# Query and key projection of a banded attention: each product once, in halves, put in place by transfers

## The chip, the cores and the metric

One NeuronCore of a Trainium2 chip runs the whole program. The metric is the device time of one execution in microseconds (us); lower is better. The kernel before took 2152.45 us, the median of three runs (2148.47 to 2153.92).

## The reference, cut to what matters

Sixteen sequences of 256 tokens with 128 features pass through eight residual blocks: a banded attention, a feed-forward net with integer weights, a causal attention, the same net, a chunked attention, a net with 4-bit block quantisation, a low-rank attention, that net again. Only the first block is touched. It has 16 heads of 64 features and a rotary embedding on queries and keys:

```
def _apply_rope(x):                       # x: (b, head, s, 64)
    cos = tile(cos(ang), (1, 2)); sin = tile(sin(ang), (1, 2))   # 32 frequencies, twice
    x1, x2 = split(x, 2, axis=-1)         # features 0..31 and 32..63 of a head
    rot = concatenate([-x2, x1], axis=-1)
    return x * cos + rot * sin
y = hidden @ W.T + bias                   # projection to 16 * 64 = 1024 features
q, k = _apply_rope(proj(Wq, bq)), _apply_rope(proj(Wk, bk)); v = proj(Wv, bv)
scores = q . k / 8, kept where the key lies in a band of 128 behind the query
out = softmax(scores) @ v, merged, @ Wo.T + bo
```

So the first 32 features of a rotated head are x1*cos - x2*sin and the other 32 are x2*cos + x1*sin.

## The kernel before, in words

**Units.** A unit is one sequence in one block; UNITS lists 16 band units (0 to 15), then 16 each of causal, chunk, lowrank and end. A unit's work is cut into steps, and the steps into six stages: forward and finish (the feed-forward net that precedes an attention), operands (norm, transpose, projections), maxima (row scores and their maximum), back (scores again, exponential, product with the values), tail (division and output projection).

**Order.** Nothing is decided on the chip. `make_plan` (from L372) goes through the steps once when the program is built, with durations from `work` (L112), dependences from `needs` (L156), a settling time for each engine (SETTLE) and, for each engine, stage and kind of unit, a number in LEAD (L292) that says how far ahead a step may push in. What comes out is one fixed list for each engine (PE, ACT, DVE, POOL, and SP, which only issues transfers), walked in order. An instruction whose wait is not met holds all that stands behind it on its engine. The plan also says which of three PSUM slots of 1024 columns (SLOTS) each product of TensorE uses; a slot comes free when the step named by `released_by` has read it.

**Operands of a band unit** (`operand_steps`, L74). The 1024 features of queries and keys are eight chunks of 128 features, two heads each. For a chunk j, step ("qk", j) makes four products of 128 x 256 into one slot: the queries, the queries with the halves of each head exchanged (from a second, permuted copy of the weights), the keys, and the exchanged keys. Each product is three matmuls, since the weights and the tokens are split into a high and a low part (`mm_split`). DVE then does four SCALAR_TENSOR_TENSOR operations (L1242): add the bias, multiply by the cosine or by the signed sine, into one of two buffers of `rope_part`; then it waits for its own writes (L1248) and frees the slot. POOL adds the two products into `band_r` (L986), in float32, ready for the scores of the back stage. ACT copies that chunk to `band_rb` in bf16 (L1007, called from the step ("cast", j)), which the row scores of the maxima stage read. ("cast", j) stands two chunks behind ("qk", j) in the list (CAST_LAG). `band_r` holds two units (RING), `band_rb` one: the first cast of a unit waits for the last row score of the unit before it. The row scores wait for all eight casts.

**After that.** Six row score products ("score", 0 to 5), each followed by a maximum on DVE (L1201); POOL turns the maxima into three bf16 parts (L937 to L940), PE transposes them, ACT copies them (nmT). The back stage has four groups of four heads: scores with the mask and the maxima added, exponential on ACT (L1087), product with the values into `ctx_ps`. In `build`, every product and mask of PE is issued by one helper, L1327, so its rows are told apart by tile names and shapes.

**SP** issues nothing during the band units; later it writes and reads back the small attentions' stacked operands through DRAM, six transfers to `scratch` (L875, L878) and four from it (L887) for each unit.

**Setup.** Before the units, the weights are loaded into buffers that are still unused, and split: ACT copies them to the high part (L730 to L737) and DVE subtracts for the low part (L757). The queries' and keys' weights are two loads of 1 MB, band_qk_a and band_qk_b, and the plain and the permuted rows stand in both.

Of the kernel before, what the change touches and what calls it, by code (L numbers as in the profile page):

```python
# [7 lines left out]
F32R = mybir.dt.float32r  # L8
# [6 lines left out]
P = 128  # L15
# [24 lines left out]
QUANT_OPS = (range(0, 3), range(3, 6), range(6, 9))  # L40
CAST_LAG = 2
# [32 lines left out]
def operand_steps(kind):  # L74

    steps = norm_steps(None)
    if kind in CONSTANT:
        steps.insert(1, ("bias",))
    if kind == "band":
        steps.insert(0, ("st",))  # L80
        for j in range(CHUNKS + CAST_LAG):
            if j < CHUNKS:
                steps.append(("qk", j))
            if j >= CAST_LAG:
                steps.append(("cast", j - CAST_LAG))
        return steps + [("v", 0), ("v", 1)]
    return steps + [("qk", 0), ("rope",), ("cast", 0), ("cast", 1), ("stack",), ("v", 0)]
# [24 lines left out]
def work(kind, step):  # L112
# [43 lines left out]
def needs(u, step, eng):  # L156
# [3 lines left out]
    if eng == "pe":  # L160
# [12 lines left out]
        if kind == "band" and step == ("qk", 0) and u >= RING:  # L173
            yield u - RING, LAST_S["band"], "pe"
        if step == ("score", 0):
            yield (u, ("stack",), "sp") if kind in SMALL else (u, ("cast", CHUNKS - 1), "act")
# [22 lines left out]
    if eng == "dve":  # L199
# [4 lines left out]
        if name == "hid":  # L204
            yield u, ("ffn", step[1]), "act"
            if step[1] == 1 and u == BATCH:
                yield u - 1, ("qk", CHUNKS - 1), "pool"
# [8 lines left out]
        if name == "qk" and step[1] >= 2:  # L216
            yield u, ("qk", step[1] - 2), "pool"
        elif name == "qk" and u:
            yield u - 1, ("qk", CHUNKS - 2 + step[1]), "pool"
# [8 lines left out]
    if eng == "act":  # L228
        if name == "low":
            yield u, ("xT", step[1]), "pe"  # L230
        if name == "cast" and kind == "band":
            yield u, ("qk", step[1]), "pool"
# [16 lines left out]
    if eng == "pool":  # L249
# [18 lines left out]
        if step == ("qk", 0) and u >= RING:  # L268
            yield u - RING, LAST_S["band"], "pe"
        if name == "clear":  # L270
            yield BATCH - 1, LAST_V["band"], "pe"
        if name == "zero":
            yield BATCH - RING, LAST_S["band"], "pe"
    if eng == "sp" and name == "stack":
# [13 lines left out]
SETTLE = {"pe": 0.18, "act": 0.12, "dve": 0.1, "pool": 0.08, "sp": 4.0}  # L288
# [5 lines left out]
        "tail": {"band": -1.574, "causal": 26.104, "chunk": 10.753, "lowrank": -0.884},  # L294
        "finish": {"causal": -2.336, "chunk": -0.206, "lowrank": -0.262, "end": -0.693},
        "forward": {"causal": 9.636, "chunk": -0.478, "lowrank": 0.173, "end": -1.16},
        "operands": {"band": 4.447, "causal": 7.702, "chunk": 18.901, "lowrank": 57.299},
        "maxima": {"band": 15.183, "causal": -0.256, "chunk": 0.135, "lowrank": -1.548},
        "back": {"band": -2.437, "causal": -0.43, "chunk": -0.634, "lowrank": -1.541},
    },  # L300
    "act": {
        "tail": {"band": 53.895, "causal": 17.872, "chunk": 17.73, "lowrank": 16.182},
        "finish": {"lowrank": -10.956, "end": -33.98},
        "forward": {"causal": -0.537, "chunk": 17.288, "lowrank": 1.988, "end": 21.987},
        "operands": {"band": -1.911, "causal": -2.563, "chunk": -3.605, "lowrank": 4.31},
        "back": {"band": 0.035, "causal": -3.733, "chunk": 11.32, "lowrank": 7.631},
    },
    "dve": {
        "tail": {"band": 24.321, "causal": 37.26, "chunk": 2.316, "lowrank": -0.51},
        "finish": {"causal": -16.196, "chunk": -16.754, "lowrank": -16.243, "end": -0.226},  # L310
        "forward": {"causal": 0.613, "chunk": 33.846, "lowrank": 11.755, "end": -4.652},
        "operands": {"band": 33.419, "causal": -10.053, "chunk": 2.99, "lowrank": 16.104},
        "maxima": {"band": 32.94, "causal": 14.633, "chunk": 16.275, "lowrank": 22.45},
    },
    "pool": {
        "tail": {"band": 8.427, "causal": 6.479, "chunk": -24.474, "lowrank": 9.213},
        "finish": {"causal": -25.627, "chunk": -19.656, "lowrank": -10.06, "end": 52.839},
        "forward": {"causal": 8.336, "chunk": -6.534, "lowrank": 23.043, "end": 42.583},
        "operands": {"band": 1.34, "causal": -30.392, "chunk": 23.562, "lowrank": 10.007},
        "maxima": {"band": 33.498, "causal": 30.314, "chunk": 6.896, "lowrank": 39.8},  # L320
    },
}
PER_UNIT = 0.01


def released_by(u, step):
# [6 lines left out]
    if name == "qk" and small:  # L333
        return u, ("rope",), "dve"
# [48 lines left out]
def make_plan():  # L383
# [8 lines left out]
    while left:  # L392
# [33 lines left out]
        done[u, step, eng] = start + time + SETTLE[eng]  # L426
# [34 lines left out]
def build(nc, a, out):  # L461
    ctx = ExitStack()
    with ctx:
# [26 lines left out]
        bias_qk = sb("bias_qk", [P, CHUNKS, 4])  # L490
        band_qk = [sb(f"band_qk{i}", [P, CHUNKS, 4, P], F32R) for i in range(2)]
# [22 lines left out]
        rope_part = sb("rope_part", [P, 2, 2, 2, TOK])  # L514
        band_r = sb("band_r", [P, RING, CHUNKS, 2, TOK])
# [72 lines left out]
        band_sum = sem("band_sum")  # L588
        band_cast = sem("band_cast")
# [77 lines left out]
        st_qk = [stage(CHUNKS * 4 * P // 2), va_flat]  # L667
# [189 lines left out]
        with nc.Block() as block:  # L857

            @block.sync
            def _(sp):  # L860
                def front_half(u, step):
# [4 lines left out]
                    if step != ("stack",):  # L866
                        return
# [862 lines left out]
```

## Time and profile before

| | |
|---|---|
| runs, us | 2152.45, 2153.92, 2148.47 |
| profiled execution, us | 2152.07 |
| its span, first to last instruction, us | 2150.2 |
| mean granted clock of TensorE | 0.936 of full speed |
| busy, share of the span | PE 83%, DVE 63%, POOL 46%, ACT 38% |
| band units | about 33 to 830 us |

The profile comes from one execution; a PE row's busy time is the union of overlapping matmuls, so a mean of one says little about the pace, and a stretch of rows in the timeline says more. PEld is the weight load beside a matmul. Rows of stretches have, in this order: the stretch and its length in us, the busy us (and instructions) of PE, PEld, DVE, ACT and POOL, the granted clock, the transfers' share and GB/s. Rows of the timeline have start and length in us, and in brackets the idle time before, with what ended it. An "issue" in a chain is time in which nothing that the profile shows was waited for.

### The profile page before, as it was taken

The numbers are of one execution on the slowest core, as the hardware profiler recorded it, in microseconds if no ns is written. First come the engines' busy times: TensorE is split into PE (matmuls) and PEld (weight loads), VectorE is DVE, ScalarE is ACT, GpSimd is POOL, SyncE is SP. The second block draws the span as 40 slices with busy tenths as digits, with TensorE's granted clock in tenths as the row PEclk, the third lists the DMA queues.
The fourth block names the chain that finished last, engine by engine and source line by source line (L and its number), as shares of the span: only waits on it lengthen the run. The fifth ranks groups of instructions, "written<-read, shape, count | busy, mean of one in ns | idle before, by whom it ended". The sixth has DMA issues, their size and how long they took to land.

```text
span 2150.2 us, 51747 instructions
## 1 busy us (share of the span) xinstructions
PE 1789.7 (83%) x21261; PEld 1250.9 (58%) x21261; DVE 1345.8 (63%) x2753; ACT 808.8 (38%) x1303; POOL 978.6 (46%) x1362
## 2 busy tenths in 40 slices
PE   4899889999999998879999997777776778888883
PEld 4566565666666666655555555667665455555553
DVE  4555555555555543574555555677876788888873
ACT  2333333333333332324444444333333444444441
POOL 3333222333332222453333435689997455555543
PEclk9999999999999999989999999888998788888886
DMA  4000000000000000023333332233443223323310
GB/s 161 1 1 1 1 2 1 1 1 1 1 1 1 1 1 1 16 56 74 64 78 71 75 75 61 60 74 78 91 87 65 46 62 65 65 65 65 65 21 8
DMA packets 167465, 89.54 MB, mean 42 GB/s; under 512 B 9393, under 2 KB 165810, under 8 KB 166978
## 3 DMA queue, kind: packets, MB, share of 16 engines
q1 hardware_dynamic: 167010, 85.70, 18.4%
q8 instruction: 172, 2.82, 0.6%
q14 instruction: 59, 0.48, 0.1%
q0 software_dynamic: 224, 0.54, 0.1%
HBM read 46.36 MB, written 39.85 MB: 40 GB/s over the span
## 4 chain that ended last, share of the span: by engine, by line
PE 51%; DVE 27%; ACT 7%; POOL 7%; issue 6%; DVEq 0%; POOLq 0%; ACTq 0%
PE slots L1327 38%; DVE nmx L1201 12%; PE ctx_ps L1327 10%; DVE rope_part L1242 4%; ACT probs L1087 3%; DVE rope_part L1166 2%; PE slots L1615 2%; ACT ctxT L1007 1%; DVE ctxT L1303 1%; DVE rope_part L1167 1%; POOL xn L922 1%; PE slots L1394 1%; ACT band_va L1023 1%; POOL band_rb L645 1%; DVE band_r L1167 1%
## 5 line engine op out<-in xcount | busy, mean ns | idle before, releaser
L1087 ACT ACTIVATE probs<-slots 128x1024 f32<-128x1024 f32 (+1 forms) x416 | 356.1, 892 | 322.0 <-PE slots L1327 318.8
L1201 DVE TENSOR_REDUCE nmx<-slots 128x8 f32<-128x1024 f32 (+2 forms) x352 | 407.7, 1216 | 102.8 <-PE slots L1327 101.2
L1327 PE MATMUL slots<-band_r 64*64 64x64 bf16 (+4 forms) x5120 | 393.6, 263 | 80.5 <-DVE nmx L1201 41.7
L1327 PEld LDWEIGHTS slots<-band_r 64*128 64x128 bf16 (+2 forms) x5120 | 194.6, 120 | 254.3 <-issue 129.8
L1242 DVE SCALAR_TENSOR_TENSOR rope_part<-slots,bias_qk,rope_band 128x256 f32<-128x256 f32 x512 | 212.3, 477 | 197.3 <-PE slots L1327 176.4
L1327 PE MATMUL ctx_ps<-probs,band_va 64*32 64x64 f32 (+4 forms) x5120 | 260.5, 313 | 42.3 <-issue 19.4
L986 POOL TENSOR_TENSOR band_r<-rope_part 128x512 f32<-128x512 f32 x128 | 164.5, 1285 | 250.9 <-DVE rope_part L1242 250.9
L1327 PE MATMUL slots<-mask,ident_bf 128*128 128x256 bf16 (+1 forms) x896 | 217.2, 324 | 46.9 <-DVE nmx L1201 17.7
L1327 PE MATMUL slots<-nmT,pick 64*128 64x256 bf16 (+2 forms) x2560 | 218.7, 241 | 2.7 <-issue 2.7
L1327 PEld LDWEIGHTS ctx_ps<-probs,band_va 128*32 128x32 f32 (+2 forms) x5120 | 145.3, 118 | 125.6 <-issue 62.8
L900 POOL TENSOR_TENSOR var_eps<-mean_var,eps 128x2 f32<-128x2 f32 x128 | 29.2, 228 | 393.4 <-DVE mean_var L1129 393.4
L1327 PE MATMUL slots<-xT,band_qk 128*128 128x256 f32 x1536 | 200.0, 288 | 8.2 <-DVEq L1248 6.1
L1327 PEld LDWEIGHTS slots<-xT,band_qk 128*128 128x128 f32 x1536 | 188.0, 191 | 19.7 <-DVEq L1248 13.6
L1007 ACT ACTIVATE ctxT<-ctx_ps 128x512 f32<-128x512 f32 (+1 forms) x112 | 87.4, 781 | 169.2 <-PE ctx_ps L1327 169.2
L922 POOL TENSOR_SCALAR band_va<-x,mean_var,rstd 128x128 f32<-128x128 f32 x128 | 100.8, 794 | 86.0 <-PE slots L1368 65.9
L1007 ACT ACTIVATE band_rb<-band_r 128x512 bf16<-128x512 f32 x128 | 79.4, 630 | 157.0 <-POOL band_r L986 157.0
L1327 PEld LDWEIGHTS slots<-mask,ident_bf 128*128 128x128 bf16 x896 | 54.9, 97 | 133.8 <-issue 44.9
L1166 DVE SCALAR_TENSOR_TENSOR rope_part<-band_va,slots 128x352 f32<-128x352 f32 (+2 forms) x128 | 68.6, 536 | 81.9 <-ACT band_va L1023 55.5
L1327 PEld LDWEIGHTS slots<-nmT,pick 64*128 64x128 bf16 (+1 forms) x2560 | 102.9, 104 | 11.5 <-issue 2.9
L922 POOL TENSOR_SCALAR xn<-x,mean_var,rstd 128x128 f32<-128x128 f32 x128 | 103.6, 816 | 2.9 <-POOL rstd L901 2.8
L937 POOL CAST nm<-nmx 128x64 bf16<-128x64 f32 x64 | 15.1, 236 | 179.0 <-PE slots L1573 92.7
L901 POOL TENSOR_TENSOR rstd<-var_eps,minus_half 128x2 f32<-128x2 f32 x128 | 91.5, 715 | 10.0
(181 smaller groups left out, 2947.5 us busy)
## 6 DMA issues: line engine op xcount, KB each, us to landing
band_r<-scratch SPq DMA_DIRECT2D x192, 192.0 KB, 4.5
scratch<-parts SPq DMA_DIRECT2D x96, 192.0 KB, 2.2
scratch<-parts SPq DMA_DIRECT2D x96, 128.0 KB, 2.1
scratch<-parts SPq DMA_DIRECT2D x96, 64.0 KB, 1.8
x<-in_x SPq DMA_DIRECT2D x16, 128.0 KB, 4.5
out<-x SPq DMA_DIRECT2D x16, 128.0 KB, 1.8
band_r<-in_band_qk_a SPq DMA_DIRECT2D x1, 1024.0 KB, 6.4
band_va<-in_band_qk_b SPq DMA_DIRECT2D x1, 1024.0 KB, 10.3
```

The costliest lines, as they stand in the source:

```text
L900: link(nc.gpsimd.tensor_tensor(var_eps[:, b], mean_var[:, b, :, 1], eps[:], ALU.add))
L901: nc.gpsimd.tensor_tensor(rstd[:, b], var_eps[:, b], minus_half[:], ALU.pow).then_inc(rstd_ready, 1)
L922: nc.gpsimd.tensor_scalar(xn[:, t, :], x[:, b, t, :], mean_var[:, b, t, 0:1], rstd[:, b, t:t + 1], ALU.subtract, ALU.mult).then_inc(xn_rea ...
L986: nc.gpsimd.tensor_tensor(band_r[:, b % RING, j], part[:, 0], part[:, 1], ALU.add).then_inc(band_sum, 1)
L1007: return nc.scalar.activation(dst, src, ACT.Copy)
L1087: nc.scalar.activation(probs[:, g % 2, step[2], :, 0:width], slot(u, step).rearrange("p (a n) -> p a n", a=2)[:, :, 0:width], ACT.Exp, sca ...
L1166: link(nc.vector.scalar_tensor_tensor(g_out, t_in, 1.0, gate, ALU.add, ALU.mult))
L1167: nc.vector.tensor_tensor(h_out, g_out, up, ALU.mult).then_inc(free_sem(u, ("ffn", i)), 1)
L1201: nc.vector.tensor_reduce(dst, src, axis=AX.X, op=ALU.max, negate=True).then_inc(free_sem(u, step), 1)
L1242: nc.vector.scalar_tensor_tensor(rope_part[:, c % 2, rot, qk, :], slot(u, step)[:, o:o + TOK], bias_qk[:, j, 2 * qk + rot:2 * qk + rot + 1 ...
L1327: return nc.tensor.matmul(o, lhsT, rhs, start=start, stop=stop, skip_group_check=shared)
L1615: last = nc.tensor.transpose(B[:, g * P:(g + 1) * P], ctxT[:, g, t * P:(t + 1) * P], ident[:])
```

## The change

**Weights and products.** The chunk of 128 features gives way to a quad of four heads (QUADS is 4). For a quad m, ("qk", m) makes four products into one slot: the first halves of the four heads' queries (4 x 32 = 128 features), the same of the keys, then the second halves of the queries and of the keys. The permuted copy of the weights is gone; the weights are one load of 1 MB.

**Rotation.** A new step ("rot", m) follows ("qk", m). In ("qk", m) DVE makes x1*cos and x2*sin and POOL subtracts; in ("rot", m) DVE makes x2*cos and x1*sin from the same slot and POOL adds. Each has four DVE operations and one of POOL, as a chunk had. The slot is freed after ("rot", m), so after eight DVE operations. POOL writes to a new buffer `quad_r`, for two quads, with 32 partitions for the half of one head.

**Transfers.** The halves lie on the wrong partitions: a head's first half belongs on partitions 0 to 31 or 64 to 95 of `band_r`, its second half 32 further. After each POOL operation, SP issues four SBUF to SBUF transfers (32 partitions, 2 KB each, 64 KB a transfer) that put them there. They count on a semaphore of their own for each of the two quad buffers. For a unit from the third on, the first half's transfers of a quad wait until the back scores S of that same group of four heads, two units earlier, have been issued by PE and are complete; before, POOL's first chunk waited for the last such group.

**Waits.** POOL reuses a quad buffer when that buffer's eight transfers of two quads before have landed. ACT's cast now covers a quad (128 x 1024), waits for its eight transfers, and stands two quads behind.

**Plan.** `work`, `needs` and `released_by` describe the new steps, SP gets 2.55 us for each group of four transfers and its own landing times (LANDS), and all 82 numbers of LEAD and PER_UNIT are new. So the lists of all five engines are drawn anew, for the other kinds of units as well, whose code is unchanged.

```diff
-        for j in range(CHUNKS + CAST_LAG):
-            if j < CHUNKS:
-                steps.append(("qk", j))
-            if j >= CAST_LAG:
-                steps.append(("cast", j - CAST_LAG))
+        for m in range(QUADS + CAST_LAG):
+            if m < QUADS:
+                steps += [("qk", m), ("rot", m)]
+            if m >= CAST_LAG:
+                steps.append(("cast", m - CAST_LAG))
...
-        "qk": [("pe", 1.43), ("dve", 1.56), ("pool", 1.21)] if big else [("pe", 0.72 if low else 1.43)],
+        "rot": [("dve", 1.56), ("pool", 1.29), ("sp", 2.55)],
+        "qk": [("pe", 1.43), ("dve", 1.56), ("pool", 1.29), ("sp", 2.55)] if big else [("pe", 0.72 if low else 1.43)],
-        "cast": [("act", 0.52)] if big else [("act", 0.52), ("pool", 1.1)],
+        "cast": [("act", 0.95)] if big else [("act", 0.52), ("pool", 1.1)],
...
-SETTLE = {"pe": 0.18, "act": 0.12, "dve": 0.1, "pool": 0.08, "sp": 4.0}
+SETTLE = {"pe": 0.18, "act": 0.12, "dve": 0.1, "pool": 0.08}
+LANDS = {"stack": 4.3, "qk": 1.4, "rot": 1.4, "res": 1.4}
 LEAD = {
     "pe": {
-        "operands": {"band": 4.447, "causal": 7.702, "chunk": 18.901, "lowrank": 57.299},
-        "maxima": {"band": 15.183, "causal": -0.256, "chunk": 0.135, "lowrank": -1.548},
+        "operands": {"band": 20.005, "causal": 1.174, "chunk": 24.896, "lowrank": 76.144},
+        "maxima": {"band": 0.021, "causal": 0.721, "chunk": 4.511, "lowrank": -1.567},
...
-PER_UNIT = 0.01
+PER_UNIT = 0.0286
...
+                    if kind == "band" and step[0] in ("qk", "rot"):
+                        m, second = step[1], step[0] == "rot"
+                        quad = b * QUADS + m
+                        sp.wait_ge(band_sum, 2 * quad + second + 1)
+                        if b >= RING and not second:
+                            sp.wait_ge(back_full, BACK_NO[u - RING, ("S", m, EXP_FILLS[kind] - 1)] + 1)
+                        for i in range(4):
+                            to = 64 * (i % 2) + 32 * second
+                            sp.dma_start(band_r[to:to + 32, b % RING, 2 * m + i // 2],
+                                         quad_r[32 * i:32 * i + 32, quad % 2, second]).then_inc(band_moved[quad % 2], 16)
...
                         pool.wait_ge(part_ready, 4 * (n + 1))
-                        if b >= RING and j == 0:
-                            pool.wait_ge(back_full, last_exp(u - RING) + 1)
+                        if quad >= 2:
+                            pool.wait_ge(band_moved[quad % 2], 128 * (quad // 2))
                         part = rope_part[:, n % 2]
-                        nc.gpsimd.tensor_tensor(band_r[:, b % RING, j], part[:, 0], part[:, 1], ALU.add).then_inc(band_sum, 1)
+                        nc.gpsimd.tensor_tensor(quad_r[:, quad % 2, second], part[:, 0], part[:, 1],
+                                                ALU.add if second else ALU.subtract).then_inc(band_sum, 1)
...
-                        act.wait_ge(band_sum, b * CHUNKS + j + 1)
+                        act.wait_ge(band_moved[quad % 2], 128 * (quad // 2 + 1))
...
-                        copy(band_rb[:, j], band_r[:, b % RING, j]).then_inc(band_cast, 1)
+                        copy(band_rb[:, 2 * m:2 * m + 2], band_r[:, b % RING, 2 * m:2 * m + 2]).then_inc(band_cast, 1)
...
+                        for sine in range(2):
                             for qk in range(2):
-                                o = 512 * qk + TOK * rot
+                                at = 2 * (second ^ sine) + qk
...
+                        if second:
+                            dve.wait_ge(part_ready, 4 * (c + 1))
+                            dve.sem_inc(free_sem(u, ("qk", m)), 1)
...
-                        pe.wait_ge(band_cast, (b + 1) * CHUNKS)
+                        pe.wait_ge(band_cast, (b + 1) * QUADS)
```

## Rows read from the trace of the kernel before

**Rows 1.** The page: each engine's busy us, share of the span, instructions.
```profile
PE 1789.7 (83%) x21261; PEld 1250.9 (58%) x21261; DVE 1345.8 (63%) x2753; ACT 808.8 (38%) x1303; POOL 978.6 (46%) x1362
```

**Rows 2.** Busy time by stretch: all band units, the rest, two single units.
```profile
33.00:830.00 797.00, 734.46 (x6694) 502.29 (x6696) 422.06 (x913) 258.06 (x397) 241.00 (x295) 0.99 0.00 1
890.00:2150.00 1260.00, 999.23 (x14144) 703.65 (x14143) 876.12 (x1727) 524.84 (x861) 701.26 (x1006) 0.90 0.30 63
...
204.50:261.05 56.55, 50.77 (x448) 34.39 (x444) 31.13 (x68) 16.96 (x27) 15.42 (x19) 0.94 0.01 1
...
472.00:522.52 50.52, 47.33 (x444) 32.38 (x440) 26.15 (x57) 16.75 (x27) 15.36 (x19) 1.00 0.00 1
```
**Rows 3.** The timeline of PE: projection of queries and keys, one unit.
```profile
472.00 8.99 PE L1327 MATMUL slots<-xT,band_qk 128*128 128x256 f32 x72
481.18 1.69 PE L1327 MATMUL slots<-xT,band_qk 128*128 128x256 f32 x12 [0.19 <-DVEq L1248]
483.05 1.68 PE L1327 MATMUL slots<-xT,band_qk 128*128 128x256 f32 x12 [0.18 <-DVEq L1248]
```

**Rows 4.** The chain of waits in order of time, from this unit's row scores on.
```profile
491.59 0.94 PE slots L1327 x10
...
492.63 4.63 DVE nmx L1201 x4
...
505.51 6.69 PE slots L1327 x60
512.20 2.24 PE ctx_ps L1327 x32
...
519.63 3.39 PE slots L1327 x30
```

**Rows 5.** Groups of instructions, 110 to 890 us: count, busy us, mean ns.
```profile
L1242 DVE SCALAR_TENSOR_TENSOR rope_part<-slots,bias_qk,rope_band 128x256 f32<-128x256 f32 x438 | 181.7, 477 | 174.4 <-PE slots L1327 156.6 <-DVE rope_part L1242 17.8
...
L986 POOL TENSOR_TENSOR band_r<-rope_part 128x512 f32<-128x512 f32 x111 | 142.6, 1285 | 220.1 <-DVE rope_part L1242 220.1
...
L1007 ACT ACTIVATE band_rb<-band_r 128x512 bf16<-128x512 f32 x111 | 68.7, 630 | 123.9 <-POOL band_r L986 123.9
```

**Rows 6.** The timeline: DVE's pace over two chunks in one unit.
```profile
155.75 1.66 DVE L1242 SCALAR_TENSOR_TENSOR rope_part<-slots,bias_qk,rope_band 128x256 f32<-128x256 f32 x4 [11.80 <-PE slots L1327]
...
157.62 1.66 DVE L1242 SCALAR_TENSOR_TENSOR rope_part<-slots,bias_qk,rope_band 128x256 f32<-128x256 f32 x4 [0.21 <-DVE rope_part L1242]
```

**Rows 7.** Waits of PE, 472 to 522.5 us: us, times, longest.
```profile
PE ctx_ps L1327 <- ACT ctxT L1007: 0.7, 1, 0.7
...
PE slots L1327 <- DVE nmx L1201: 0.4, 2, 0.2
...
PE slots L1327 <- DVEq L1248: 0.4, 2, 0.2
```

**Rows 8.** SP's transfers by line: ns of one issue, smallest, median, largest.
```profile
L875 SPq DMA_DIRECT2D scratch<-parts x144: 360/489/1875, 878.5 to 2037.5; - x144
...
L887 SPq DMA_DIRECT2D band_r<-scratch x192: 537/617/1665, 925.0 to 2047.4; - x192
```

**Rows 9.** The page's transfer issues: count, KB each, median us to landing.
```profile
band_r<-scratch SPq DMA_DIRECT2D x192, 192.0 KB, 4.5
...
scratch<-parts SPq DMA_DIRECT2D x96, 64.0 KB, 1.8
```
**Rows 10.** Busy time by stretch, after and around a gap of PE.
```profile
235.00:238.00 3.00, 1.08 (x14) 0.59 (x10) 0.51 (x3) 1.02 (x1) 2.66 (x6) 1.00 0.00 0
238.00:241.00 3.00, 2.28 (x26) 1.36 (x25) 1.34 (x3) 1.25 (x3) 0.53 (x1) 0.87 0.00 0
241.00:245.00 4.00, 3.80 (x17) 1.67 (x15) 1.57 (x3) 0.00 (x0) 0.00 (x0) 0.50 0.02 4
245.00:248.00 3.00, 3.00 (x19) 3.00 (x20) 0.00 (x0) 1.02 (x1) 0.00 (x0) 0.66 0.00 0
```

**Rows 11.** The setup, DVE's timeline: the second load's low part.
```profile
15.88 2.29 DVE L757 TENSOR_TENSOR band_qk<-band_va,band_qk 128x2048 fp32r<-128x2048 f32 x1 [1.39 <-ACT band_qk L734]
```

More of the change, by code:

```diff
@@ L40 @@
 QUANT_OPS = (range(0, 3), range(3, 6), range(6, 9))
+QUADS = HEADS // 4
 CAST_LAG = 2
@@ L172, in needs @@
             yield u, ("low", False), "dve"
-        if kind == "band" and step == ("qk", 0) and u >= RING:
-            yield u - RING, LAST_S["band"], "pe"
         if step == ("score", 0):
-            yield (u, ("stack",), "sp") if kind in SMALL else (u, ("cast", CHUNKS - 1), "act")
+            yield (u, ("stack",), "sp") if kind in SMALL else (u, ("cast", QUADS - 1), "act")
         if name == "nm":
@@ L303 @@
[L303 to L306, printed above, removed]
+        "tail": {"band": 35.697, "causal": 34.402, "chunk": 10.557, "lowrank": 26.695},
+        "finish": {"lowrank": -5.609, "end": -20.226},
+        "forward": {"causal": 13.82, "chunk": 38.078, "lowrank": -16.965, "end": 37.732},
@@ L307 @@
+        "operands": {"band": 1.828, "causal": -3.97, "chunk": -2.376, "lowrank": 8.411},
+        "back": {"band": -29.994, "causal": -5.221, "chunk": 4.729, "lowrank": -20.078},
     },
     "dve": {
[L309 to L312, printed above, removed]
@@ L313 @@
-        "maxima": {"band": 32.94, "causal": 14.633, "chunk": 16.275, "lowrank": 22.45},
+        "tail": {"band": -1.733, "causal": 60.397, "chunk": 5.011, "lowrank": 19.119},
+        "finish": {"causal": -48.899, "chunk": -28.059, "lowrank": 0.492, "end": -16.236},
+        "forward": {"causal": -4.349, "chunk": 70.344, "lowrank": 25.847, "end": -54.899},
+        "operands": {"band": -2.503, "causal": -6.955, "chunk": 5.379, "lowrank": 33.812},
+        "maxima": {"band": -2.962, "causal": -51.183, "chunk": 30.291, "lowrank": 36.608},
@@ L314 @@
     },
     "pool": {
[L316 to L320, printed above, removed]
-    },
-}
-PER_UNIT = 0.01
+        "tail": {"band": -42.083, "causal": 40.938, "chunk": 0.066, "lowrank": 6.629},
@@ L326, in released_by, with settles @@
+        "finish": {"causal": -27.454, "chunk": -49.756, "lowrank": 9.302, "end": 76.825},
+        "forward": {"causal": 1.399, "chunk": -20.38, "lowrank": 19.311, "end": 52.875},
+        "operands": {"band": 6.442, "causal": -8.743, "chunk": 50.085, "lowrank": 11.974},
+        "maxima": {"band": 8.799, "causal": 24.457, "chunk": -6.764, "lowrank": 62.179},
+    },
+}
+PER_UNIT = 0.0286
+def settles(step, eng):
+    return LANDS[step[0]] if eng == "sp" else SETTLE[eng]
 def released_by(u, step):
@@ L588, in build @@
         band_sum = sem("band_sum")
+        band_moved = [sem(f"band_moved{i}") for i in range(2)]
         band_cast = sem("band_cast")
@@ L685, in build @@
         }
-        def qk_half(part, i):
-            half = CHUNKS // 2
-            return band_qk[part][:, i * half:(i + 1) * half].rearrange("p a b c -> p (a b c)")
         def loaded(eng, *names):
```

91 lines of the change are left out of this document (43 added, 48 removed).

## The prediction

> **What bounds the kernel now.** I read first the busy shares, then busy time by stretch, then PE's timeline and the chain inside one unit. The page puts PE at 83% of the span and DVE at 63% [rows 1], but that averages unlike stretches. In the 797 us of the band units PE is busy 734.5 us (92%), DVE 422 (53%), POOL 241, ACT 258; in the 1260 us from 890 on PE is busy 79% and DVE 70% [rows 2]. So PE sets the pace in the first part, and in the second no single engine does. Most band units repeat to 0.02 us: from 421 to 725 us six periods of 50.5 us follow each other, and the one from 472.00 has PE busy for 47.33 us of 50.52, DVE for 26.15, at full clock [rows 2]. Three units that also carry the quantisation of the 4-bit weights are longer, the one from 204.50 by 6 us.
>
> Inside a period the reader is to see two things. The projection is one solid block of PE: 72 matmuls in 8.99 us, then twice 12 in 1.69 us behind a wait of 0.19 for a slot that DVE frees [rows 3], from 472.00 to 484.73, 12.7 us in all. Six chunks of 12 matmuls in 8.99 us are 1.50 us a chunk. And the chain runs over DVE only in this block and in the row scores, where 0.94 us of PE are followed by 4.63 us of maxima; from 505.5 to the period's end it is PE alone, back to back [rows 4]. What PE does less is therefore time won, as long as something else is ready to be put in its place.
>
> **Products removed.** Half the matmuls of the projection go: 4 quads x 12 in place of 8 chunks x 12, 16 units x 48 = 768 in all. The block of 12.7 us becomes 4 x 1.50 = 6.0 us of PE work [rows 3], so a period can shorten by 6.7 us at most, 107 us over 16 units. That is the bound of the gain in the band units.
>
> **DVE, POOL, ACT.** DVE makes as many operations of the same shape as before, 32 a unit at 0.477 us; POOL eight of 1.285 us, now four subtractions among them, which I price as the additions; ACT four casts of 1024 columns in place of eight of 512 at 0.630 us [rows 5]. Two of the old make 1.26 us, which bounds the new cast above, and one, 0.63, bounds it below; I take 1.05 us, so ACT gains about 0.8 us a unit. ACT is idle two thirds of a period [rows 2], so that is worth nothing. DVE's pace stays 1.87 us for each four operations, 155.75 to 157.62 [rows 6], 15.0 us for a unit. This is now 2.5 times PE's 6.0 us, where it was 1.2 times: the products can no longer be issued in one block, PE has to do about 9 us of other work between them. The back stage of the unit before offers enough: a period has 47.3 - 6.7 = 40.6 us of PE work, of which 34.6 is not this projection.
>
> **New hand-overs.** Breaking the block up costs small waits. The rows show what one is worth: 0.2 us for a slot released by DVE, 0.7 us for a `ctx_ps` bank that ACT copies out, at most [rows 7]. A quad holds its slot for eight DVE operations, 3.7 us, where a chunk held it for 1.7, so with three slots one or two are left for the back stage while the rotation runs. I take four more waits of 0.2 and one of 0.7, 1.5 us a unit. Below it is 0 (the planner finds an order without them), above it is the 6.7 us that is gained. So 6.7 - 1.5 = 5.2 us a unit is won, and a period becomes 45.3 us.
>
> **Transfers.** Each unit gets 8 groups of 4 transfers on SP, 512 in all, 33.6 MB. SP has nothing else to do in the band units; behind these transfers stand only the later ones of the same kind. An issue holds SP for 0.489 us (to DRAM) or 0.617 us (from it, more descriptors) in the median, 0.36 to 1.88 in all [rows 8]. I take 0.6: a group is 2.4 us and a unit 19.7 us by the larger median, 11.5 by the smallest row, 60 by the longest. At 19.7 SP is busy 43% of the new period, but inside the rotation it is slower than DVE (15.0 us). A 64 KB transfer to DRAM landed 1.8 us after issue, 192 KB in small rows from DRAM after 4.5 [rows 9]; SBUF to SBUF isn't in the trace, and I take 2.1, near the nearer row in size, with 0.6 and 4.5 as ends. The first sum is done 1.5 + 0.2 + 1.9 + 1.3 = 4.9 us after the first product starts; then 19.7 us of issues, 1.5 until the last has landed and a cast of 1.05 make 27 us to the first row score, where it was 491.59 - 472.00 = 19.6 [rows 3, 4]. That is 7.5 us more latency, and it costs nothing while PE has the unit before to work on: in those 27 us it needs 27 - 6.0 - 3.3 (two value projections of 1.66 us) = 18 us of other work, and the period has over 25 left without the row scores. With that cover gone it would cost 7.5 us a unit. If the transfers land late by 1 us, ACT waits in front of its exponentials; half of that might reach PE, one time a unit: 0.5 us, inside the 1.5 above.
>
> The trace shows what a real hole would add: where PE was busy only 1.08 of 3 us, the granted clock stood at 0.87, then 0.50 and 0.66 in the next stretches before it was back at 1.00, that is 1.2 GHz for some 6.8 us with PE busy throughout [rows 10]. Those matmuls took up to twice their time, so it cost up to 3.4 us. The Trainium skill (TensorE: Matmul & The Clock Gate, HAM oscillation) says that waits which come back in each round of a loop can throttle the array again every time. By that rule a transfer wait in every unit would pay those 3.4 us every time, 51 us over 15 units; by the periods of before, at 1.00 with no gap over 0.7 us [rows 2, 7], nothing. I keep it out of the sum and make it a rival (F).
>
> **Start.** One load of 1 MB, ACT's copy and DVE's subtraction of 2.29 us with 1.39 us of waiting before it fall away [rows 11]. They stand on the way to the first unit: 2.3 to 3.7 us, I take 3. The first unit has no unit before it to hide the longer rotation, so I count its 5.2 us as not won; the other 15 units count.
>
> **Later units.** Their code is unchanged but all lists are drawn anew. PE has 1260 - 999 = 261 us idle there [rows 2]; nothing in the trace says whether the new order has more or less. I take 0 and, as bounds, 2% of the stretch either way, 25 us.
>
> **The sum.** 15 x 5.2 + 3 = 81 us. The profiled execution took 2152.07 us with a span of 2150.2, 0.4 us from the median of 2152.45: 2152 - 81 = 2071 us.
>
> **Rivals.** A, the forecast: PE sets the pace, a period of 44.5 to 47 us; 2045 to 2100.
> B, the longer rotation is only partly covered. For it: SP and DVE both outlast PE in this block, and three slots are few. Against it: 25 us of other work are there. If a third of the 7.5 us shows, 2.5 us a unit, the gain is 15 x 2.7 + 3 = 43, 2109 us (2095 to 2130).
> C, more than forecast: no new waits (6.7 us a unit, 100 + 3) or a better order later: 2049 from the first alone, 2035 with some of the second.
> D, slower: SP becomes the bound. One mechanism: each unit needs 32 issues in order, and rotation can't run ahead by more than two quads. From 50.5 / 32 = 1.58 us an issue on, SP alone takes longer than the period of before. By the longest row of the loads, 1.665 us, it would be 53.3 us, 15 x 2.8 = 42 us more, 2191. Against it: medians of a third of that.
> E, the change doesn't shorten the period, because DVE's chain of 15.0 + 6.9 (maxima) and the waits between them set it already: 2149. Against it: PE is busy 94% of the period and the last 17 us of the chain are PE alone.
> F, the clock: PE waits once a unit for a cast whose transfers are late, long enough for the clock to fall as it did after the gap of before: 3.4 us at the most in each of 15 units [rows 10], on top of the forecast: 2122. Against it: such a gap has to be several times as long as any in a steady unit now. (It is the rule of the clock page above.)
>
> **How the numbers follow.** A 0.65, B 0.13, C 0.10, D 0.07, F 0.03, E 0.02. This kernel's runs differ by up to 0.3%, 6.5 us; less can't be told from no change. The range of 2038 to 2120 takes all of A, two thirds of B and most of C; it leaves out D, E, F and the rest, some 0.18. Faster by over 0.3%: A, B, C and F, 0.91; within 0.3%: E, 0.02; slower: D, 0.07.
>
> **What would show it.** In the profile of after: 768 matmuls on band_qk in groups of 12, each 1.5 us apart from other PE work; a steady period near 45.3 us with PE busy about 41 and the clock at 1.00; SP issues of 0.5 to 0.65 us, 512 of them, landing in 1.5 to 2.5 us; POOL waiting for transfers seldom; the first row score some 27 us behind the first product of its unit. Wrong would be: a period above 47 us with PE idle for a cast or a slot (B), issues above 1.5 us (D), a stretch after the last band unit whose length differs from before by more than 25 us, or a clock below 1.00 in the steady units.

## The result, and the profile after

The changed kernel takes 2123.3 us (median of 2124.22, 2130.74, 2122.37 and 2122.23), against 2152.42 before: a ratio of 0.9869, 95% interval 0.9848 to 0.9891. Faster by 1.3%, where 3.8% was forecast, and 3 us above the range.

The page of after, to be read against [rows 1]: PE is busy for 58 us less, and its clock is lowered in the first two slices, where the page of before has 9. (In the later units it is lowered in both, and a 9 is anything from 0.90 on, so this row can't show the 0.93 to 0.96 of the band units below.)

```profile
span 2122.0 us, 50629 instructions
...
PE 1731.3 (82%) x20493; PEld 1184.8 (56%) x20493; DVE 1345.2 (63%) x2752; ACT 788.8 (37%) x1238; POOL 972.0 (46%) x1362
...
PEclk8799999999999999999999999987877788888897
```

Time went where the tiles' first starts show it. PE's rows of the projections of two kinds of unit, in the trace of before and then of after (min/median/max ns, first and last start):

```profile
L1327 PE MATMUL slots<-xT,causal_qkv x192: 276/281/387, 857.7 to 1244.0; 128*128 128x256 f32 x192
...
L1327 PE MATMUL slots<-xT,lowrank_qkv x96: 274/281/562, 1610.9 to 2023.8; 128*128 128x256 f32 x96
```
```profile
L1342 PE MATMUL slots<-xT,causal_qkv x192: 276/280/387, 828.6 to 1211.6; 128*128 128x256 f32 x192
...
L1342 PE MATMUL slots<-xT,lowrank_qkv x96: 277/281/553, 1571.0 to 2000.6; 128*128 128x256 f32 x96
```

The first causal unit starts 29.1 us earlier. From there to the end of the span before has 1292.5 us and after 1293.4, so the new order of the later units is worth nothing in sum (they win 11 us up to the first lowrank unit and lose them again). 2.8 of the 29.1 us are the setup, and 26.3 the band units. The same stretch, first product to first causal product, in busy time by engine (stretch and length, busy us of PE, PEld, DVE, ACT, POOL, clock, transfers); first before, then after, and after's first 67 us alone:

```profile
33.13:857.70 824.57, 755.12 (x6847) 519.20 (x6847) 436.24 (x950) 265.04 (x413) 251.95 (x311) 0.99 0.00 1
33.13:103.37 70.24, 61.58 (x487) 43.12 (x487) 42.43 (x86) 21.81 (x32) 28.99 (x34) 1.00 0.00 1
```
```profile
30.37:828.60 798.23, 684.62 (x6107) 445.62 (x6107) 436.05 (x950) 252.95 (x351) 249.56 (x311) 0.93 0.18 43
30.37:97.04 66.67, 36.91 (x184) 24.70 (x184) 35.18 (x80) 12.93 (x15) 27.68 (x30) 0.73 0.27 64
```

This is the whole account. PE lost 768 matmuls of 0.125 us (1.50 us for 12), 96.0 us of work, but its busy time fell by only 70.5. The other 25.5 us, a remainder, I put down to matmuls at the lower clock: in e9 below, whose steady units are at 1.00, PE is busy 684.1 us in this stretch with 240 added matmuls of about 0.11 us, so some 658 without them, and there the 96 us are gone in full. And PE's idle time rose from 69.5 to 113.6 us, by 44.2. 96.0 - 25.5 - 44.2 = 26.3 us. Half of the new idle time, 21.1 us, lies in the first two units; the other 14 have 23.1, or 1.65 us each.

**A steady unit after.** It takes 47.56 us (50.52 before), with PE busy 42.28 at a clock of 0.96 where [rows 2] had 47.33 at 1.00. The projection is no block any more: three quads, the first back scores of an older unit, the fourth quad, then the rest of that back stage. PE's timeline, cut to the ends of its parts (561.75 is the first row score of the unit whose projection began at 487.39):

```profile
534.95 4.50 PE L1342 MATMUL slots<-xT,band_qk 128*128 128x256 f32 x36
540.06 0.28 PE L1588 MATMUL slots<-ident_bf,nm 128*128 128x128 bf16 x2 [0.61 <-DVEq L1263]
...
544.63 1.69 PE L1342 MATMUL slots<-xT,band_qk 128*128 128x256 f32 x12
...
561.75 0.61 PE L1342 MATMUL slots<-mask,ident_bf 128*128 128x512 bf16 x2
...
569.28 0.27 PE L1588 MATMUL slots<-ident_bf,rd 128*128 128x128 bf16 x2 [0.37 <-DVE rd L1225]
570.11 0.49 PE L1342 MATMUL slots<-rdT,wide_pick 64*128 64x256 bf16 x4 [0.56 <-ACT rdT L1019]
571.18 0.28 PE L1342 MATMUL slots<-rdT,wide_pick 64*128 64x256 bf16 x2 [0.58 <-DVE ctxT L1318]
...
572.38 1.03 PE L1342 MATMUL slots<-mask,ident_bf 128*128 128x512 bf16 x2 [0.32 <-DVE ctxT L1318]
573.35 0.61 PE L1342 MATMUL slots<-band_rb 64*128 64x256 bf16 x4
573.88 3.79 PE L1342 MATMUL slots<-band_v,xT 128*128 128x512 f32 x12
...
578.92 3.84 PE L1342 MATMUL slots<-band_o,ctxT 128*128 128x128 f32 x32 [1.03 <-ACT band_va L1019]
```

From 543.5 to 566.6 PE runs without a gap. Of the 5.3 us of holes 1.9 lie before that and 3.4 at the unit's end, and there are two things there, side by side. First, the division (den, rden, scale) is a chain over PE, DVE and ACT, and from rden on nothing lies between its steps. In the kernel before, back scores of the next unit lay between rd and rdT, and behind them:

```profile
502.71 0.29 PE L1573 MATMUL slots<-ident_bf,rd 128*128 128x128 bf16 x2
502.83 0.38 PE L1327 MATMUL slots<-mask,ident_bf 128*128 128x256 bf16 x2
503.14 0.49 PE L1327 MATMUL slots<-band_r 64*128 64x128 f32 x4
...
503.85 0.28 PE L1327 MATMUL slots<-rdT,wide_pick 64*128 64x256 bf16 x2
...
505.51 0.61 PE L1327 MATMUL slots<-mask,ident_bf 128*128 128x512 bf16 x2 [0.25 <-DVE ctxT L1303]
```

The clock answers. Busy time by stretch of the unit after:

```profile
565.72:568.90 3.18, 2.96 (x24) 0.93 (x20) 2.08 (x5) 0.87 (x2) 0.00 (x0) 1.00 0.27 63
568.90:572.38 3.48, 1.33 (x12) 0.55 (x11) 3.31 (x6) 0.38 (x1) 0.00 (x0) 0.96 0.02 5
572.38:575.00 2.62, 2.62 (x9) 1.19 (x10) 2.62 (x3) 0.94 (x1) 0.00 (x0) 0.50 0.00 0
```

PE is busy 1.33 of 3.48 us, and then stands at 0.50 (1.2 GHz): the mask product of two matmuls takes 1.03 us, where others take 0.6. It is the picture of [rows 10], now in every steady unit, though no single gap here is longer than 0.58 us. Second, ACT's four casts, since they wait for the last row score of the unit before, all start there, and the two value copies stand behind them, for which the output product's slot waits 1.03 us (ACT's timeline):

```profile
574.06 3.90 ACT L1019 ACTIVATE band_rb<-band_r 128x1024 bf16<-128x1024 f32 x4 [4.09 <-PE slots L1342]
577.86 1.92 ACT L1019 ACTIVATE band_va<-slots 128x1024 f32<-128x1024 f32 x2
```

**The transfers** cost what was forecast: an issue holds SP for 0.591 us in the median, and they land 2.0 us after. In this unit SP issues its 32 from 544.78 to 566.68, seven us before the casts start. POOL does wait for landings, where I had forecast that it would seldom: 31 times and 129.0 us in all, in the steady unit too (6.01 us at 551.69). But there PE has other work; only in the first two units does nothing hide the wait. The transfers' rows by their line, then SP's timeline of the first two units, then POOL's in the steady unit and in the first:

```profile
L875 SPq DMA_DIRECT2D band_r<-quad_r x512: 507/591/1780, 36.4 to 755.7; - x171
...
  POOL quad_r L997: 129.0, 31
...
DMA to landing us min/median/max: 1.9/2.0/3.7
```
```profile
36.38 53.76 SPq L875 DMA_DIRECT2D band_r<-quad_r  x64
```
```profile
551.69 2.50 POOL L997 TENSOR_TENSOR quad_r<-rope_part 128x512 f32<-128x512 f32 x2 [6.01 <-DMA band_r<-quad_r]
```
```profile
48.38 2.48 POOL L997 TENSOR_TENSOR quad_r<-rope_part 128x512 f32<-128x512 f32 x2 [2.90 <-DMA band_r<-quad_r]
```

### The profile page after: what moved, and what is told of

It is laid out like the page before. It is cut to its first block, busy times and chain, and to the rows that moved or that the text cites. A ratio compares the mean times of both kernels' runs of the same rounds, so it can differ in the third digit from the quotient of the medians.

```text
span 2122.0 us, 50629 instructions
## 1 busy us (share of the span) xinstructions
PE 1731.3 (82%) x20493; PEld 1184.8 (56%) x20493; DVE 1345.2 (63%) x2752; ACT 788.8 (37%) x1238; POOL 972.0 (46%) x1362
## 4 chain that ended last, share of the span: by engine, by line
PE 55%; DVE 23%; ACT 9%; issue 6%; POOL 4%; SPq 1%; DMA 0%; DVEq 0%; POOLq 0%; ACTq 0%
PE slots L1342 39%; PE ctx_ps L1342 11%; DVE nmx L1214 8%; DVE rope_part L1256 5%; ACT probs L1100 3%; PE slots L1630 2%; DVE rope_part L1179 2%; DVE ctxT L1318 1%; ACT ctxT L1019 1%; SPq L875 1%; DVE band_r L1180 1%; ACT band_va L1019 1%; ACT band_rb L1019 1%; PE slots L1383 1%; DVE rope_part L1180 1%
## 5 line engine op out<-in xcount | busy, mean ns | idle before, releaser
L1342 PE MATMUL slots<-band_r 64*64 64x64 bf16 (+4 forms) x5120 | 398.9, 268 | 62.7 <-DVE nmx L1214 38.1
L997 POOL TENSOR_TENSOR quad_r<-rope_part 128x512 f32<-128x512 f32 x128 | 162.5, 1279 | 285.3 <-DVE rope_part L1256 156.2
L1342 PE MATMUL slots<-mask,ident_bf 128*128 128x256 bf16 (+1 forms) x896 | 224.0, 333 | 65.4 <-DVEq L1263 20.4
L1256 DVE SCALAR_TENSOR_TENSOR rope_part<-slots,bias_qk,rope_band 128x256 f32<-128x256 f32 x512 | 206.4, 476 | 101.5 <-POOL quad_r L997 74.3
L1342 PE MATMUL slots<-nmT,pick 64*128 64x256 bf16 (+2 forms) x2560 | 225.7, 252 | 0.0
L911 POOL TENSOR_TENSOR var_eps<-mean_var,eps 128x2 f32<-128x2 f32 x128 | 29.2, 228 | 268.2 <-DVE mean_var L1142 267.6
L1342 PEld LDWEIGHTS slots<-mask,ident_bf 128*128 128x128 bf16 x896 | 54.6, 98 | 151.4 <-issue 45.3
L1155 DVE TENSOR_TENSOR xT<-slots,xT 128x256 fp32r<-128x256 f32 x64 | 27.0, 422 | 137.2 <-ACT xT L1019 137.2
L1342 PEld LDWEIGHTS slots<-nmT,pick 64*128 64x128 bf16 (+1 forms) x2560 | 108.8, 115 | 9.1
L1342 PE MATMUL slots<-xT,band_qk 128*128 128x256 f32 x768 | 103.1, 292 | 4.1 <-ACT probs L1100 2.8
L1019 ACT ACTIVATE band_rb<-band_r 128x1024 bf16<-128x1024 f32 x64 | 62.9, 1046 | 106.9 <-PE slots L1342 74.8
L1342 PEld LDWEIGHTS slots<-xT,band_qk 128*128 128x128 f32 x768 | 97.0, 197 | 9.0 <-ACT probs L1100 3.7
```

What stands on the lines that cost most here:

```text
L911: link(nc.gpsimd.tensor_tensor(var_eps[:, b], mean_var[:, b, :, 1], eps[:], ALU.add))
L997: nc.gpsimd.tensor_tensor(quad_r[:, quad % 2, second], part[:, 0], part[:, 1], ALU.add if second else ALU.subtract).then_inc(band_sum, 1)
L1019: return nc.scalar.activation(dst, src, ACT.Copy)
L1155: nc.vector.tensor_tensor(lo[:], slot(u, ("xT", ahead))[:, 0:TOK], hi[:], ALU.subtract).then_inc(free_sem(u, ("xT", ahead)), 1)
L1256: nc.vector.scalar_tensor_tensor(rope_part[:, c % 2, sine, qk, :], slot(u, ("qk", m))[:, at * TOK:(at + 1) * TOK], bias_qk[:, m, at:at + 1 ...
L1342: return nc.tensor.matmul(o, lhsT, rhs, start=start, stop=stop, skip_group_check=shared)
```

## The experiments

All ratios are to the kernel before on the same chip. "Steady period" is the distance of the first projection product from unit to unit, in the steady units.

**e1, one transfer a group.**

```diff
-for i in range(4):
-    to = 64 * (i % 2) + 32 * second
-    sp.dma_start(band_r[to:to + 32, b % RING, 2 * m + i // 2], quad_r[32 * i:32 * i + 32, quad % 2, second])
+sp.dma_start(band_r[:, b % RING, 2 * m + second], quad_r[:, quad % 2, second])
```

> The changed kernel, but each group of four 64 KB transfers is one straight transfer of 128 partitions to band_r (same bytes; the halves stay where they are, so the scores are of other numbers). 128 issues on SP in place of 512. The order lists are those of the changed kernel. Theory O (the drawn order and the chain over PE, DVE and ACT set the period of 47.6 us; the transfers end before the casts that wait for them): POOL's waits for transfers shrink, the period stays 47.3 to 47.6 us, 2115 to 2125 us. Theory T (22 us of issues on SP and the landings hold the unit): the period falls toward 45.4 us, 2095 us or less.

2109.5 us, ratio 0.9796 (0.9774 to 0.9817). Neither expectation held: the steady period is 47.6 us, as theory O said, but the time is lower. The second and third unit start 25.6 and 30.2 us behind their forerunners, where the changed kernel needs 33.4 and 33.3, 10.9 us together. So within the band units the issues cost time in the fill alone (the third unit gives 2.0 back). The traces' spans differ by 12.3 us, and 3.6 of them come behind the first causal unit, where both kernels have the same transfers; that part stays unexplained.

**e2, the removed products alone.** The kernel before, `for i in (0, 2)` in place of `range(4)`, DVE reading the plain product twice.

> The kernel before with its own order, but without the products of the exchanged halves: 6 matmuls a chunk in place of 12, DVE reads the plain product twice (so the rotation is wrong). No transfers. This is the removed TensorE work alone, 768 matmuls. If PE work removed is time won whatever the order, 2152 - 80 to 100 = 2050 to 2070 us. If the order has to be drawn anew (DVE's 15.0 us of rotation stand between the first product and the row scores, and PE's list has nothing to put there), the period stays 50 to 50.5 us with PE's busy time down by some 5 us: 2140 to 2152 us.

2155.2 us, ratio 0.9994 (0.9975 to 1.0012): nothing. The projection is as in the rows of its PE timeline, 6 matmuls each behind a wait for DVE's slot; the last row is the unit's first row score:

```profile
469.22 0.97 PE L1327 MATMUL slots<-xT,band_qk 128*128 128x256 f32 x6 [0.47 <-DVEq L1248]
471.10 0.98 PE L1327 MATMUL slots<-xT,band_qk 128*128 128x256 f32 x6 [0.90 <-DVEq L1248]
472.97 1.65 PE L1327 MATMUL slots<-xT,band_qk 128*128 128x256 f32 x6 [0.90 <-DVEq L1248]
...
485.94 0.59 PE L1327 MATMUL slots<-mask,ident_bf 128*128 128x512 bf16 x2
```

Every 1.88 us one chunk: DVE's pace. It stays the same where the clock falls and six matmuls take 1.65 us (the unit's first 17.6 us have 0.81). The first row score stands 19.6 us behind the unit's first product at 466.37, exactly as in the kernel before [rows 3, 4]. The unit takes 50.5 us as before, with PE busy for only 2.4 us less, where 6.0 went: the rest went into the clock, 0.93 over the unit, and into the loose ends of groups of 6. Up to the first causal unit this trace has 817.9 us in place of 824.6, and it loses half of that again later. The same work taken from PE gives 6.7 us before the later units in one order and 26 us in another.

**e3, the old numbers of the order in the changed kernel.**

> The changed kernel with the 82 numbers of LEAD and PER_UNIT of the kernel before; everything else as changed. Theory O (the order decides): well above the changed kernel, 2170 to 2210 us. If the new steps bring their gain under any reasonable order, 2115 to 2135 us.

2267.3 us, ratio 1.0519 (1.0484 to 1.0554), worse than expected; steady period 55 to 57 us. The new numbers are part of the change, not an addition to it.

**e4, dummy matmuls in the slots,** of 512 bf16 columns, just behind the step's own `take`.

```diff
+if kind == "band" and name in ("rden", "scale"):
+    warm(B, {"rden": 2, "scale": 2 if step == ("scale", 0) else 1}[name])
```

> The changed kernel with dummy bf16 matmuls of 512 columns (128x128 weights), two before the rden transposes, two before the first scale product and one before each other of a band unit, written to the slot that the real product then overwrites. They lie where PE waits (1.33 us busy of 3.48 us before the clock falls). If the lowered clock behind this gap costs its full 1.7 us in each of 15 units: clock back at 1.00, 2098 us. If the slowed matmuls are mostly covered by ACT's chain (four casts and two value copies, 574.06 to 578.9 in the unit from 534.95), only the last row score's delay of 0.6 us counts: 2113 us. If the dummies don't hold the clock: 2123 us or somewhat more.

2115.6 us, ratio 0.9818 (0.9800 to 0.9835). The clock of a steady unit is back at 1.00, and its period stays 47.57: in that unit the output product now waits 1.74 us for ACT's value copy, where it waited 1.03. The dummies also cost: they lengthen the division's chain, so that the last row score starts 38.1 us behind the unit's first product (520.28 - 482.19), where it was 37.4 at the lower clock, and the casts start 39.1 us behind it in both. The gain comes from the three units with quantisation (49.5 us in place of 51.5) and a few others.

**e5, a second buffer for the casts.** `band_rb2` for odd units; ACT waits for the row scores of unit u - 2.

> The changed kernel with a second band_rb buffer: ACT's casts of a unit wait for the row scores of two units before, not of the unit before; the order lists are unchanged. In the steady unit the four casts (3.9 us) start at 574.06, when the last row score is done, and the two value copies and the output product's slot wait behind them (1.03 us of PE). Theory A (this chain of ACT ends the period): the casts start at 570, behind rdT, the value copies are no longer late, the period falls from 47.6 to 46.5 us: 2105 to 2110 us. If another wait takes its place (the row scores wait for DVE anyway): 2119 to 2123 us.

2120.3 us, ratio 0.9821 (0.9795 to 0.9848). ACT's casts start behind rdT, the wait for the value copy is gone, and the periods become unequal. Stretches of single units in its trace:

```profile
486.69:532.88 46.19, 41.99 (x396) 27.17 (x394) 25.80 (x57) 16.03 (x22) 15.13 (x19) 0.96 0.20 47
579.32:626.83 47.51, 43.37 (x396) 28.18 (x394) 25.80 (x57) 16.02 (x22) 15.11 (x19) 0.93 0.19 46
```

The same instructions, 46.2 us at a clock of 0.96 and 47.5 at 0.93. By these rows what ACT's wait had hidden is the clock; e9 puts it to the test.

**e6 and e7, orders drawn anew.** The durations in `work` (many of PE's, a few of ACT's and, in e6, SP's) set to the traces' and LEAD and PER_UNIT searched again, for the changed kernel and for the one before.

> The changed kernel with a redrawn order: PE's durations in `work` set to what the trace shows (1.50, 1.66, 0.87, 1.82 and 1.13 us and so on), SP's group 2.72 us, and new numbers in LEAD. Nothing else is changed. Theory O (the order decides what is left of the removed work): faster than the changed kernel by 1 to 4%, 2040 to 2100 us. If the period is bound by something that an order can't move: 2115 to 2125 us.

> The kernel before with an order redrawn in the same manner and with as long a search as e6. It tells apart what belongs to the new order and what to the removed work: if the changed steps are worth 96 us of PE work wherever the order is good, e6 is 40 to 90 us below this kernel; if e6 gains only because orders were searched better, both lie close. Expected: 2110 to 2150 us, period 50.5 us as before, since PE's list is nearly full.

2114.9 us, ratio 0.9811 (0.9787 to 0.9836), and 2171.8, ratio 1.0065 (1.0043 to 1.0088). Both expectations were too good. The steady periods are 47.8 and 51.2 us, no better than with the old numbers; against the changed kernel e6 wins 5.5 us up to the first causal unit, loses 21.6 from there to the first lowrank unit, and wins 25.5 behind it (525.5 us in place of 551.0). e6 is 57 us below e7, inside the 40 to 90 us that were to show the changed steps' worth; but e7 is slower than the order that the kernel before already had, so this gap doesn't show what the steps are worth. The plan has no clock in it, and no second buffer, so a search in it can't find what e9 finds.

**e8, each product twice.** `for i in [0, 1, 2, 3] * 2`.

> The changed kernel with each product of the projection made twice (24 matmuls a quad, the second overwrites the first with the same numbers): TensorE's work is again that of the kernel before, in the new order. If PE's work bounds the new order, +6.2 us a unit: 2215 us. If the holes of PE (5.3 us a unit) take part of it, mainly at the waits for slots that DVE frees: 2150 to 2190 us. If PE isn't the bound at all: 2123 us.

2177.9 us, ratio 1.0095 (1.0070 to 1.0119); the steady period is 51.2 us, 3.6 more for 6.0 us of work. It isn't work alone that has changed: the clock of these units is back at 1.00, and PE is busy 46.4 us where it was 42.3, 4.1 more. So some 1.9 of the missing 2.4 us are the clock that the added work itself brings back, and 0.5 are holes filled. In the new order PE's work does set the period, all but for such holes; in the old one (e2) it did not.

**e9, both causes away.** e5's buffer, and dummies in a place that holds no slot:

```diff
+def warm(n):
+    for _ in range(n):
+        mm(ctx_ps[:, 1, TOK:2 * TOK], ident_bf[:], mask[:], True, True, shared=True)
...
+if kind == "band" and name in ("rden", "scale"):
+    warm(3)
 B = take(u, step)
```

> The changed kernel with both: the second band_rb buffer of e5, and dummy bf16 matmuls of 256 columns (0.11 us each, three before each of the five slot takes of rden and scale) into columns of ctx_ps that no band step reads, so that no slot is held. Two waits lie side by side at the end of the steady unit: ACT's casts (1.03 us) and the lowered clock behind the gap (3 to 6 us at 1.2 GHz, so 1.5 to 3 us). In e4 and e5 only one was taken away and the steady period stayed 47.6, or 46.2 to 47.6. Theory C (two parallel causes, each hides the other): the period falls to 44.9 to 45.3 us, clock 1.00 in the steady units, 2080 to 2095 us against 2123 of the changed kernel. If a third wait stands beside them: 46.5 us or more, 2110 us.

2090.4 us, ratio 0.9709 (0.9681 to 0.9737). A steady unit:

```profile
471.63:516.64 45.01, 42.52 (x410) 27.70 (x409) 25.91 (x57) 16.02 (x22) 15.12 (x19) 1.00 0.20 48
```

**e12, the dummies alone,** as in e9 but with one buffer.

> The changed kernel with the dummies of e9 (into free columns of ctx_ps, no slot held) and its one band_rb buffer: the fourth corner beside the changed kernel (steady period 47.6), e5 (46.2 to 47.6) and e9 (45.0). Theory C: the tail of the unit ends some 1.5 us earlier, so the casts start earlier too, but ACT's 3.9 us of casts and 1.9 us of copies still stand behind the last row score: period 46.3 to 47.0 us, clock 1.00, 2100 to 2112 us. If the clock alone was the cause: 45.0 to 45.5 us, as e9. If it counts for nothing without the buffer: 47.6.

2109.3 us, ratio 0.9772 (0.9737 to 0.9808), steady period 47.0. Its waits of PE over three units (us, times, longest) have ACT's copies at their head:

```profile
PE slots L1342 <- ACT band_va L1019: 5.2, 3, 1.8
```

That completes the square: steady period 47.6 with neither, 46.2 to 47.6 with the buffer, 47.0 with the dummies, 45.0 with both. Each alone wins at most 1.4 us, both 2.6. From the first product to the first causal unit the buffer alone wins 4.0 us, the dummies alone 15.0, both 31.9.

**e10 and e11, the fill.** e9 with e1's single transfer, and e9 where ACT issues half of the transfers of the first two units ahead of its casts:

```diff
+for second in range(2 if u < 2 else 0):
+    act.wait_ge(band_sum, 2 * quad + second + 1)
+    for i in (2, 3):
+        to = 64 * (i % 2) + 32 * second
+        nc.scalar.dma_start(band_r[to:to + 32, b % RING, 2 * m + i // 2],
+                            quad_r[32 * i:32 * i + 32, quad % 2, second]).then_inc(band_moved[quad % 2], 16)
```

> e9 with the one straight transfer a group of e1 (the scores are of other numbers). Theory F (the transfers cost time in the first two units only, where no other unit covers them): 8 to 12 us below e9 before the first causal unit, and the same period. If the transfers have become the next bound of the shorter period: 20 us or more below e9.

> e9 where ACT issues half of the transfers of units 0 and 1 (16 of 32 each), ahead of its casts, and SP the other half; the later units as in e9. By theory F the second unit's first product starts some 5 to 8 us earlier, and the end 4 to 8 us below e9: 2075 to 2090 us. If the landing and not the issue holds the first units: as e9.

2075.6 us, ratio 0.9644 (0.9614 to 0.9673), and 2083.9, ratio 0.9688 (0.9650 to 0.9726). Both steady periods are 45.0. The first causal unit starts 15.8 us earlier than in e9 (expected 8 to 12; 11.9 of them in the first two units, the rest in a few later ones that fall in with the rhythm sooner), and 10.4 us earlier with two queues. By its median e11 is the fastest kernel here that leaves nothing out: 3.1% below the kernel before and 1.8% below the changed one. Against e9 the intervals overlap; that it is faster rests on its trace.

## Why the prediction was wrong

**The direction and the terms that held.** PE's work does set the pace in the new order (e8), though in the old one DVE's chain stood beside it (E, below); a quad costs 1.50 us; DVE, POOL and ACT have the forecast durations (cast 1.05 us, in the page 1.046); SP's issue 0.59 us (0.6 taken) and landing 2.0 us (2.1 taken); setup 2.8 us (3 taken); later units 0.9 us (0 taken).

**The steps that failed** are the two that the sum left bare. The larger is the clock, put at nothing: "I keep it out of the sum and make it a rival (F)." The other is the fill: "The first unit has no unit before it to hide the longer rotation, so I count its 5.2 us as not won; the other 15 units count." Over all 16 units the sum had 107.2 us of work away and 29.2 of waits (16 x 1.5 and 5.2), 78 in all. Measured are 96.0 away, 44.2 of idle time added and 25.5 of lowered clock, 26.3 in all. The difference of 51.7 us is 25.5 from the clock; 12.9 from the waits of the first two units (21.1 where 8.2 stood in the sum); 11.2 from the work, since a unit loses 6.0 us of matmuls, and my 6.7 took the old block's own waits and loose ends for work; and 2.1 from the waits of the other 14 units.

That these last came out at 1.65 us a unit for the 1.5 taken is luck. The terms were four waits for a slot from DVE and one for a bank that ACT copies; what the trace has in their place is the division's chain and, longest, 1.03 us behind ACT's casts.

I gave rival F 0.03, since "such a gap has to be several times as long as any in a steady unit now". That reason was wrong. In the kernel before a single gap of 0.7 us left the clock at 1.00; in the unit after, five gaps of 0.3 to 0.6 us stand close together, PE is busy 1.33 of 3.48 us, and the granted clock falls to 0.50. And the back scores that lay between the division's steps in the unit from 472.00 were part of the very work that was to move between DVE's rotations. I had counted that cover (25 us of other work for the rotation, 18 needed) and not asked what it leaves bare where it comes from.

The Trainium skill (TensorE: Matmul & The Clock Gate, HAM oscillation) says that a wait in each round of a loop throttles the array again each time. The trace after agrees, with 0.50 behind the gap of each steady unit. The wait is for DVE and ACT, though, not for transfers. That F's number, 2122 us, is 1 us from the measured time is luck too: F had 51 us of clock on top of a forecast that held otherwise, and there are 25.5.

**Rival B** was right about the size of the period (47.6 us, "above 47 us with PE idle for a cast or a slot") and wrong about the cause: no transfer is late for a cast in a steady unit (e1). What B should have named is the order of ACT's list: casts behind the last row score, value copies behind the casts. I had expected the first row score 27 us behind its unit's first product. In the first unit it is 30.4 us, but in a steady one 74.4 (487.39 to 561.75): the new order puts a unit's row scores behind the next unit's projection. That hides the rotation's latency whole, and with one `band_rb` it pins that next unit's casts to the period's end.

**The first units.** What was worth 5.2 us to me is 21.1 us of PE's idle time over two units, and the low clock there (0.73 where it was 1.00). The longer latency, which I had worked out, falls on each unit that nothing covers, and there are two of them. The waits of PE from 30 to 98 us (us, times, longest):

```profile
PE slots L1383 <- POOL xn L933: 10.9, 2, 8.5
PE slots L1342 <- DVEq L1263: 9.6, 6, 2.5
PE slots L1342 <- ACT band_va L1019: 9.3, 2, 6.4
```

In e1's first two units these are 7.5, 10.4 and 0.8 us. So what the issues cost is the wait for the value copies, which stand behind casts that wait for transfers, and a third of the wait for POOL. What stays is the slot that is held for eight DVE operations (1.4 us of such waits before), and POOL's list; neither was taken away in a run.

**D, E.** Issues never held a steady unit. E, that DVE's chain sets the period, had 0.02 and was right of the order of before: in e2 that chain keeps the first row score at 19.6 us and the period at 50.5, with 6.0 us of PE's work gone. PE's busy share of 94% had hidden it. It is not right of the new order, where row scores come a period later: e9 reaches 45.0 us with the same DVE work. That is also the period that I had forecast, two changes late: 45.3.

## What to carry to other kernels

Where work is moved to cover a new wait, look at the place that it leaves: its old neighbours may be a chain that it alone had covered. Where a wait disappears and the time doesn't move, look for a second wait that ends at the same point, and take both away before either is called harmless. A high busy share doesn't say that an engine's work is the time: another engine's chain can be as long. And work taken from the busiest engine is worth what the order makes of it: here, up to the first later unit, 7 us (e2), 26 us (the change), or 58 us (e9: 766.3 us in place of 824.6, dummies included).

## What the runs showed of the hardware

The granted clock fell to 0.50 behind a stretch in which PE was busy 1.33 of 3.48 us and no single gap was longer than 0.58 us. Work that does nothing can pay: 15 bf16 matmuls of 256 columns a unit, PE time of its own, held the granted clock at 1.00 and, with the buffer, took the period from 46.2 to 47.6 us down to 45.0. And what a transfer from SBUF to SBUF cost its queue did not grow with its size here: 64 KB over 32 partitions took 0.591 us to issue, 256 KB over 128 partitions took 0.466 (landing after 2.4 us in place of 2.0). One for four made the fill of two units 10.9 us shorter. The row of e1:

```profile
L873 SPq DMA_DIRECT2D band_r<-quad_r x128: 464/466/1330, 36.0 to 741.0; - x128
```
